# Layer one's tables: when the lists are loaded and made, and how the Q and P products are laid out

## The chip, the cores and the metric

The kernel runs on one core of a Trainium2 chip. The metric is the device time of one execution, in microseconds. The core has five engines that run their own instruction streams beside each other: TensorE (PE, matmuls and transposes into the eight PSUM banks), VectorE (DVE), ScalarE (ACT), GpSimd (POOL) and SyncE (SP, which here only issues DMAs). ACT and POOL issue DMAs as well. Streams meet only at semaphores.

## The reference

Two graph layers on 6250 nodes with 128 features and 206,250 edges sorted by destination. What matters here is layer one:

```python
h = x @ W1 + b1                                   # per node
e = concat([h[dst], h[src] - h[dst]])             # per edge
m = relu(e @ W2 + b2)
m = relu(m @ W3 + b3)
out = relu(segment_max(m, dst))
x = layernorm(x + out)
# layer two: per edge logit from dst and src, softmax over the edges of a node,
# weighted sum of projected rows, an MLP, a norm over the nodes, then
x = layernorm(x + layer_two(x, src, dst))
```

`e @ W2` splits into a part that depends on the destination alone and a part that depends on the source alone. So the kernel makes two tables of one row per node, P (for destinations, bias included) and Q (for sources), and an edge needs relu(P[dst] + Q[src]).

## The kernel before

**Tables (the first 80 us).** x is loaded in 13 steps of 512 rows (`load_x`, L280) by SP and ACT. For each step PE transposes four 128x128 blocks (`tr_x`, L763), ACT copies the result out of PSUM into one of two buffers `xTs` (L531), and PE multiplies it by a folded 128x256 weight `Wf`, whose left half gives P and right half Q (`mm_pq`, L772). DVE adds the bias on the way out of PSUM, four instructions of 128x256 for each step: Q goes to one of four buffers `qs`, P to its place in the large tile `accT` (`ev_pq`, L1064). SP stores Q step by step (L336), then P (L340). `accT` is later the accumulator of the layer, and is cleared at L1099.

**Lists.** The edges are cut into 1612 tiles of 128. `src` is loaded into S0 and `dst` into D, both with 124 partitions and 13 columns of 128 numbers (L458 to L460, L478 to L482, issued by POOL). DVE makes from D: `rel` (the place in the tile's window of 128 nodes), flags where a node starts and ends, `relend`, and five lists of bf16 numbers `metaS[0..4]` (L1074 to L1090). The lists go to DRAM (`lists_out`, L294: five stores, each 124 x 13 runs of 256 bytes; k = 0, 1 by SP, 2, 3, 4 by ACT). PE also turns three lists (`tr_list`, L782) and ACT keeps them in `srcT`, `relT`, `endT` (L537). `srcT` holds the indices of POOL's gathers.

**The edge loop.** 403 groups of four tiles. POOL gathers the Q rows of a tile (L489), SP loads the window of P for a tile (`windows`, L362) and, at two places of every 13 groups, spreads lists 0 and 1 over 128 partitions (`spread`, L368). PE adds both in PSUM (L806, L807), ACT applies relu, PE multiplies by W3 (L814), DVE runs a segmented maximum (L1110), PE picks the ends (L822, L831) and DVE adds into `accT` (L1128). SP enters the loop only after `meta_out` has reached 80 (all five lists stored), both tables are stored and all transposes of lists are done. Group k of POOL may run at most 13 groups ahead of PE.

Each engine's order is written by hand: `in_turn` runs stages step by step. In the first phase the order on DVE is: all 13 steps of `ev_pq` (with one cast of src behind step 2), then all the work on D, then the clearing of `accT`.

## Time and profile before

| what | value |
|---|---|
| median of 3 runs | 5077.51 us (5074.24 to 5079.42) |
| span of the profiled execution | 5109.1 us |
| busy: PE, POOL, DVE, ACT | 3054.7, 3094.9, 2392.0, 1577.1 us |
| first matmul of the edge loop | 125.46 us after the span's start |

The profiled execution is the only one that has a trace; the span from its first to its last instruction is 31.6 us longer than the median of the runs, so profiling adds some 0.6%. Times below are counted from the span's start. A row of the timeline gives start, duration, engine, line and operation, tiles, shape and count; the square brackets say how long the engine stood idle before and what ended that. A row whose engine ends in q (SPq, ACTq) is the engine's sequencer issuing a DMA: while it lasts nothing else of that engine's stream goes on. A DMA's landing is a separate time.

### The profile page before, as it was taken

How to read it: one execution, taken by the hardware profiler on the slowest of the kernel's cores; microseconds unless marked ns; L12 is line 12 of the kernel's file. 1: busy time of each engine (PE TensorE's matmuls, PEld its weight loads, DVE VectorE, ACT ScalarE, POOL GpSimd, SP SyncE). 2: the span in 40 equal slices, each digit the busy share in tenths (PEclk: the TensorE clock that was granted, in tenths of full speed). 3: DMA queues.
4: the chain of work that ended last, by engine and by line, in shares of the span. 5: the costliest groups of instructions: out<-in, count | busy, mean ns of one | idle time of the engine just before them, and what ended most of it. 6: DMA issues, size and time to landing. Idle time of an engine off the chain costs nothing.

```text
span 5109.1 us, 59978 instructions
## 1 busy us (share of the span) xinstructions
PE 3054.7 (60%) x16577; PEld 2440.6 (48%) x16577; DVE 2392.0 (47%) x7924; ACT 1577.1 (31%) x2413; POOL 3094.9 (61%) x3251
## 2 busy tenths in 40 slices
PE   3687777877777777777843444434444444444456
PEld 2566565666566665666612433333333333333343
DVE  3355444544544454444613444434444444444456
ACT  1344434444344444444522212212122221212214
POOL 4666666666666666666255666666666666666630
PEclk7888888888888898888865556666655555656567
DMA  6444444444444444444222222222222222222221
GB/s 154 133 138 134 130 128 140 134 127 133 138 129 124 146 132 125 141 129 131 81 77 58 68 74 69 75 68 68 75 67 75 68 68 74 68 71 72 68 67 53
DMA packets 407860, 512.07 MB, mean 100 GB/s; under 512 B 102789, under 2 KB 323495, under 8 KB 407527
## 3 DMA queue, kind: packets, MB, share of 16 engines
q1 hardware_dynamic: 292374, 288.47, 17.5%
q0 software_dynamic: 104832, 216.49, 17.1%
q10 hardware_dynamic: 10322, 3.28, 0.4%
q8 instruction: 135, 2.21, 0.2%
q14 instruction: 197, 1.61, 0.1%
HBM read 492.20 MB, written 15.68 MB: 99 GB/s over the span
## 4 chain that ended last, share of the span: by engine, by line
another core or an unknown queue 33%; PE 26%; issue 21%; ACT 10%; DVE 9%; DVEq 1%; DMA 1%; ACTq 1%; SPq 0%
PE bank L814 6%; PE bank L807 6%; PE bank L831 5%; DVE Z L1285 3%; PE bank L806 3%; PE bank L822 3%; ACT Z L639 2%; ACT Z L575 1%; PE bank L928 1%; ACT Z L570 1%; DVE Z L1274 1%; ACT Z L646 1%; DVE accT L1128 1%; ACT Z L582 1%
## 5 line engine op out<-in xcount | busy, mean ns | idle before, releaser
L489 POOL DMA_INDIRECT G<-q_tab,srcT x1612 | 1535.2, 952 | 892.1 <-issue 413.9
L489 POOL DMA_INDIRECT G<-x_tab,srcT x832 | 793.2, 953 | 478.1 <-issue 232.9
L1128 DVE TENSOR_TENSOR accT<-accT,bank 128x128 f32 x1612 | 454.5, 282 | 1166.6 <-remote 922.0
L489 POOL DMA_INDIRECT X<-x_tab,srcT x780 | 744.7, 955 | 380.3 <-issue 221.8
L807 PE MATMUL bank<-Z 128*128 128x128 f32 x3224 | 682.4, 308 | 103.0 <-issue 100.9
L928 PE MATMUL bank<-Z,G 128*128 128x128 f32 x1664 | 380.1, 396 | 554.4 <-DVE Z L1285 238.4
L928 PE MATMUL bank<-Z,X 128*128 128x128 f32 x1560 | 370.1, 406 | 523.1 <-DVE Z L1274 181.3
L1285 DVE SCALAR_TENSOR_TENSOR Z<-Z,evr,bank 128x128 f32 x1612 | 551.2, 342 | 195.4 <-issue 138.3
L807 PEld LDWEIGHTS bank<-Z 128*128 128x128 f32 x3224 | 576.9, 221 | 128.1 <-issue 127.8
L831 PE MATMUL bank<-Z 128*128 128x128 f32 x3224 | 520.9, 295 | 174.2 <-issue 168.4
L814 PE MATMUL bank<-Z,W3s 128*128 128x512 f32 x806 | 522.6, 736 | 156.1 <-issue 135.0
L928 PEld LDWEIGHTS bank<-Z,G 128*128 128x128 f32 x1664 | 323.0, 287 | 601.0 <-issue 411.2
L1274 DVE TENSOR_SCALAR Z<-iota,relT,evr 128x128 f32<-128x128 f32 x1612 | 563.6, 362 | 90.8 <-ACT evr L669 52.3
L806 PE MATMUL bank<-ident,G 128*128 128x128 f32 x1612 | 489.3, 304 | 165.3 <-issue 139.7
L928 PEld LDWEIGHTS bank<-Z,X 128*128 128x128 f32 x1560 | 314.1, 296 | 566.4 <-issue 317.7
L831 PEld LDWEIGHTS bank<-Z 128*128 128x128 f32 x3224 | 456.7, 209 | 189.0 <-issue 184.6
L1110 DVE TENSOR_TENSOR_SCAN Z<-Z,bank 128x512 f32<-128x512 bf16 x403 | 513.3, 1274 | 71.2 <-PE bank L814 66.7
L582 ACT ACTIVATE Z<-bank 128x512 f32<-128x512 f32 x403 | 239.6, 594 | 915.5 <-remote 651.9
L1116 DVE TENSOR_SCALAR Z<-iota,endT 128x128 f32<-128x128 f32 x1612 | 438.1, 296 | 0.0
L589 ACT COPY Z<-bank 128x512 f32<-128x512 f32 x403 | 234.5, 582 | 486.4 <-remote 298.2
L822 PEld LDWEIGHTS bank<-ident,Z 128*128 128x128 f32 x1612 | 237.0, 161 | 275.8 <-issue 274.6
L806 PEld LDWEIGHTS bank<-ident,G 128*128 128x128 f32 x1612 | 257.5, 160 | 209.6 <-issue 209.0
(198 smaller groups left out, 2982.5 us busy)
## 6 DMA issues: line engine op xcount, KB each, us to landing
Z<-p_tab SPq DMA_DIRECT2D x1612, 64.0 KB
Z<-meta SPq DMA_DIRECT2D x62, 896.0 KB
Z<-meta SPq DMA_DIRECT2D x61, 832.0 KB
Z<-meta SPq DMA_DIRECT2D x62, 768.0 KB
G<-q_tab,srcT POOLq DMA_INDIRECT x1612
G<-x_tab,srcT POOLq DMA_INDIRECT x832
X<-x_tab,srcT POOLq DMA_INDIRECT x780
x_tab<-X SPq DMA_DIRECT2D x13, 264.0 KB, 2.0
```

The costliest lines, as they stand in the source:

```text
L489: return pool.indirect_dma_start(to, None, of, bass.IndirectOffsetOnAxis(ap=srcT[:, t:t + 1], axis=0))
L806: nc.tensor.matmul(o, G[:, g * GT + j, 0:F], ident[:, :], start=True, stop=False, is_transpose=True)
L807: last = nc.tensor.matmul(o, Pwin[:, g * GT + j, :], OH[k % 3][:, j * 128:(j + 1) * 128], start=False, stop=True)
L814: nc.tensor.matmul(bank[2 + k % 2][:, :], W3s[:, :], M1[k % 3], start=True, stop=True).then_inc(v_mm, 1)
L822: last = nc.tensor.transpose(bank[4 + k % 2][:, j * 128:(j + 1) * 128], S[k % 3][:, j * 128:(j + 1) * 128], ident[:, :])
L831: last = nc.tensor.matmul(bank[6 + k % 2][:, j * 128:(j + 1) * 128], STs[k % 3][:, j * 128:(j + 1) * 128], EOH[k % 3][:, j, :], start=True ...
L928: last = nc.tensor.matmul(sum_bank(n)[:, j * 128:(j + 1) * 128], ring(t)[:, 1:F + 1], EW[n % (AHEAD + 1)][:, j, :], start=True, stop=True)
L1110: v.tensor_tensor_scan(out=S[k % 3], data0=bc[:, 1, g * CH:(g + 1) * CH], data1=bank[2 + k % 2][:, :], initial=NEG if k == 0 else S[(k - 1 ...
L1116: made = v.tensor_scalar(EOH[k % 3][:, j, :], iota_w, endT[:, k * GT + j:k * GT + j + 1], None, ALU.is_equal)
L1128: v.tensor_tensor(win, win, bank[6 + k % 2][:, j * 128:(j + 1) * 128], ALU.add).then_inc(acc_ok, 1)
L1274: made = v.tensor_scalar(EW[n % (AHEAD + 1)][:, j, :], iota_w, relT[:, t:t + 1], evr[:, q % 2, 0, at:at + 1], ALU.is_equal, ALU.mult)
L1285: v.scalar_tensor_tensor(out=win, in0=win, scalar=evr[:, q % 2, 1, w:w + 1], in1=sum_bank(n)[:, j * 128:(j + 1) * 128], op0=ALU.mult, op1= ...
```

## The change

- POOL no longer loads src at the start. It makes its constants first, then waits for x steps 0 to 6 and 8 (SP's) and 3 and 5 (ACT's), then loads src, then dst, then the 15 small weights that ACT loaded before.
- ACT copies every turned step of x into `accT` and keeps it there (`xt_of`); `xTs` is gone.
- PE makes 13 Q products (the right half of `Wf`) behind the transposes, then 13 P products (the left half) from the kept x. Four PSUM banks hold one product each.
- DVE takes each product out in one instruction of 128x512 into one of the four buffers `qs`; P uses the same buffers. SP stores all 26 in order.
- The work on D and S0 is cut into six pieces, each put behind one of the 26 steps of `ev_pq`. One tile `edge` holds the flags of starts and ends; ACT makes lists 0, 1, 2 and 4 from DVE's results, and subtracts 1 from `relend` when it keeps `endT`.
- ACT alone stores the five lists, in the order 0, 1, 2, 3, 4, between its other work.
- SP loads the `base` numbers before the stores of tables. It waits for the P stores one by one in the first 13 groups of windows, not for all ahead of the loop.

```diff
-            in_turn(STEPS, [(0, store_q)])
             with nc.allow_non_contiguous_dma(reason="one number for each tile"):
                 sp.dma_start(base[:, 0:TILES - 1], ...)
-            in_turn(STEPS, [(0, store_p)])
-            sp.wait_ge(prep, 6)
-            lists_out(sp, (0, 1))
+            def store(i):
+                tab, h = (q_tab, p_tab)[i // STEPS], i % STEPS
+                sp.wait_ge(pq_ev, i + 1)
+                sp.dma_start(tab[h * CH:(h + 1) * CH, :].rearrange("(p b) f -> p b f", b=SB), qs[i % 4]).then_inc(pq_out[i % 4], 16)
+
+            in_turn(2 * STEPS, [(0, store)])
             sp.wait_ge(meta_out, 80)
             sp.wait_ge(base_in, 32)
-            sp.wait_ge(p_out, 16 * STEPS)
 ...
             def windows(k, g):
+                if k < STEPS:
+                    sp.wait_ge(pq_out[(STEPS + k) % 4], (STEPS + k) // 4 * 16 + 16)
 ...
-            x_ready(pool, X_SP[-2])
-            x_ready(pool, X_ACT[-1])
+            pool.wait_ge(pads, 4)
+            x_ready(pool, X_SP[4])
+            x_ready(pool, X_ACT[1])
+            pool.dma_start(S0[0:ROWS, 0:COLS - 1, :], src[0:end].rearrange("(c p e) -> p c e", p=ROWS, e=T)).then_inc(src_in, 16)
 ...
+            pool.dma_start(W3s[:, :], W3[:, :]).then_inc(weights_in, 16)
 ...
                 act.wait_ge(xt_tr, h + 1)
-                after(act, pq_mm, h - 1)
-                nc.scalar.copy(xTs[h % 2], bank[h % 2][:, :]).then_inc(xt_cp, 1)
+                nc.scalar.copy(xt_of(h), bank[h % 2][:, :]).then_inc(xt_cp, 1)
 ...
+            act.wait_ge(prep, 2)
+            nc.scalar.copy(metaS[R, 0], rel[R]).then_inc(meta_ok, 1)
+            act.wait_ge(prep, 3)
+            nc.scalar.mul(metaS[R, 1], edge[R, :, 0:T], NEG).then_inc(meta_ok, 1)
+            act.wait_ge(meta_ok, 2)
+            lists_out(act, (0, 1))
+            nc.scalar.mul(metaS[R, 2], edge[R, :, 1:T + 1], NEG).then_inc(meta_ok, 1)
+            keep_list(1, lambda c, o: nc.scalar.copy(relT[:, c], o))
+            act.wait_ge(meta_ok, 3)
+            act.wait_ge(prep, 5)
+            lists_out(act, (2, 3))
             act.wait_ge(prep, 6)
-            lists_out(act, (2, 3))
-            act.wait_ge(prep, 7)
+            nc.scalar.copy(metaS[R, 4], S0[R]).then_inc(meta_ok, 1)
+            act.wait_ge(meta_ok, 4)
             lists_out(act, (4,))
+            keep_list(2, lambda c, o: nc.scalar.activation(endT[:, c], o, ACT.Identity, bias=minus))
 ...
-            in_turn(STEPS, [(0, tr_x), (1, mm_pqs)])
-            tr_list(rel, 1, 2)
-            tr_list(relend, 2, 5)
+            in_turn(STEPS, [(0, tr_x), (1, products)])
+            for i in range(STEPS, 2 * STEPS):
+                product(i)
+                if i == STEPS + 4:
+                    tr_list(rel, 1, 2)
+            tr_list(relend, 2, 4)
 ...
+            between = {6: numbers, 9: places_in_windows, 11: new_nodes, STEPS + 2: ends_of_nodes, STEPS + 5: other_nodes, STEPS + 8: places_in_blocks}
+
+            def ev_pq(i):
+                dve.wait_ge(pq_mm, i + 1)
+                after(dve, pq_out[i % 4], i // 4 * 16)
+                o = (128, 0)[i // STEPS]
+                v.tensor_tensor(qs[i % 4], blocks(bank[2 + i % 4][:, :]), bias[:, o:o + 128].unsqueeze(1).broadcast_to([128, SB, 128]), ALU.add).then_inc(pq_ev, 1)
+                if i in between:
+                    between[i]()
```

The new functions: `numbers` waits for src and casts it; `places_in_windows` waits for dst and makes `rel`; `new_nodes` makes `edge`; `ends_of_nodes` makes `relend`; `other_nodes` makes list 3 and `contS`; `places_in_blocks` masks dst for list 4. `product(i)` waits until product i - 4 has been taken out. `keep_list(n, keep)` is the old one with the instruction passed in; list 0 is now kept behind step 9 of x and not step 7.

How the instructions move on DVE, from the first product to the end of the work on the lists. Before, the last steps and what follows them (`Z<-bank` is an eviction to a Q buffer, `accT<-bank` one of P, `Z<-Z` the work on D and S0):

```order
L1064 TENSOR_TENSOR Z<-bank,brow 128x256 [waits q_out0,pq_mm]
L1064 TENSOR_TENSOR Z<-bank,brow 128x256
L1064 TENSOR_TENSOR accT<-bank,brow 128x256 x2
L1074 TENSOR_TENSOR Z<-Z 124x1664 [waits dst_in]
L1075 TENSOR_TENSOR Z<-Z 124x1664
L1077 CAST Z<-Z 124x1664 [waits prep,turns_dve]
L1078 TENSOR_SCALAR Z<-Z 124x1664
L1079 TENSOR_SCALAR Z<-Z 124x1664
L1081 TENSOR_SCALAR contS<-Z 124x13 [waits turns_dve]
```

Now, from step 6 to step 12 of the Q products:

```order
L1103 TENSOR_TENSOR Z<-bank,brow 128x512 [waits pq_out2,pq_mm]
L1075 CAST Z<-Z 124x1664 [waits src_in]
L1103 TENSOR_TENSOR Z<-bank,brow 128x512 [waits pq_out3,pq_mm]
L1103 TENSOR_TENSOR Z<-bank,brow 128x512 [waits pq_out0,pq_mm]
L1103 TENSOR_TENSOR Z<-bank,brow 128x512 [waits pq_out1,pq_mm]
L1079 TENSOR_TENSOR Z<-Z 124x1664 [waits dst_in]
L1103 TENSOR_TENSOR Z<-bank,brow 128x512 [waits pq_out2,pq_mm]
L1103 TENSOR_TENSOR Z<-bank,brow 128x512 [waits pq_out3,pq_mm]
L1082 TENSOR_TENSOR Z<-Z 124x1677
```

The work on dst stood behind all evictions, and now its first piece (L1079) stands ahead of the last three Q evictions and all those of P. The evictions are half as many and twice as wide.

On ACT, what stands between the last copy of x and the edge loop. Before:

```order
L531 COPY Z<-bank 128x512 [waits pq_mm,xt_tr] x5
L545 DMA W3s<-in_L_gnn_W 128x128
L550 DMA wprojs<-in_L_gnn_w_proj 127x128
...
L537 COPY relT<-bank 128x496 [waits list_tr] x3
L537 COPY relT<-bank 128x124 [waits list_tr]
L537 COPY endT<-bank 128x496 [waits list_tr] x3
L537 COPY endT<-bank 128x124 [waits list_tr]
L294 DMA meta<-Z 124x13x128 [waits prep]
L294 DMA meta<-Z 124x13x128
L294 DMA meta<-Z 124x13x128 [waits prep]
```

Now:

```order
L540 COPY accT<-bank 128x512 [waits xt_tr] x3
L556 CAST Z<-Z 124x1664 [waits prep]
L558 ACTIVATE Z<-Z 124x1664 [waits prep]
L295 DMA meta<-Z 124x13x128 [waits meta_ok]
L295 DMA meta<-Z 124x13x128
L561 ACTIVATE Z<-Z 124x1664
L562 COPY relT<-bank 128x496 [waits list_tr] x3
L562 COPY relT<-bank 128x124 [waits list_tr]
L295 DMA meta<-Z 124x13x128 [waits prep,meta_ok]
L295 DMA meta<-Z 124x13x128
L567 CAST Z<-Z 124x1664 [waits prep]
L295 DMA meta<-Z 124x13x128 [waits meta_ok]
```

The 15 loads of weights have gone to POOL. All five stores of lists stand on ACT, and the copies of `relT` stand behind the first two of them.

On POOL, the loads of src stood at its start. Now, behind its constants:

```order
L470 MEMSET X 128x52x3
L474 DMA Z<-in_src 124x12x128 [waits x_in3,x_in4,pads]
L475 DMA Z<-in_src 123x128
L476 DMA Z<-in_src 1x14x3
L477 DMA Z<-in_dst 1x3x43
L478 DMA Z<-in_dst 123x130
L479 DMA Z<-in_dst 124x11x130
L480 DMA Z<-in_dst 123x130
L481 DMA Z<-in_dst 1x43
L482 DMA W3s<-in_L_gnn_W 128x128
```

src and dst are now neighbours in one queue, and the loads of weights follow them.

## Rows read from the trace of the kernel before

**Rows 1.** The page: its span, and the group of POOL's gathers in layer one.
```profile
span 5109.1 us, 59978 instructions
L489 POOL DMA_INDIRECT G<-q_tab,srcT x1612 | 1535.2, 952 | 892.1 <-issue 413.9
```
**Rows 2.** Busy us in a stretch: PE, PEld, DVE, ACT, POOL; PE's granted clock.
```profile
1000.00:2000.00 1000.00, 770.83 (x4369) 610.02 (x4368) 494.04 (x1512) 408.02 (x671) 636.34 (x672) 0.87 0.45 133
```
**Rows 3.** The chain that ended last, to 130 us: start, duration, what.
```profile
3.95 21.66 DMA X<-in_x
...
128.26 15.34 issue
```
**Rows 4.** Timeline: work on lists, their stores, SP's next DMAs, the first matmul.
```profile
57.65 1.88 DVE L1074 TENSOR_TENSOR Z<-Z 124x1664 f32<-124x1664 int32 x1
...
72.91 15.12 SPq L294 DMA_DIRECT2D meta<-Z  x2
73.03 25.19 ACTq L294 DMA_DIRECT2D meta<-Z  x2
...
110.66 0.82 SPq L368 DMA_DIRECT2D Z<-meta  x2
...
125.46 0.45 PE L806 MATMUL bank<-ident,G 128*128 128x128 f32 x1 [52.80 <-issue]
```
**Rows 5.** Busy us in two stretches; the last number is DMA in GB/s.
```profile
8.00:10.00 2.00, 0.09 (x1) 0.00 (x0) 0.00 (x0) 1.50 (x2) 0.88 (x8) 1.00 1.18 311
...
12.00:14.00 2.00, 2.00 (x10) 1.68 (x9) 0.75 (x2) 0.61 (x2) 0.00 (x0) 1.00 1.41 116
```
**Rows 6.** Timeline: POOL's loads of src and dst, and the cast of src.
```profile
2.19 2.81 POOL L458 DMA_DIRECT2D Z<-in_src  x1 [0.65 <-DVE brow L1047]
...
34.53 1.05 DVE L1068 CAST Z<-Z 124x1664 f32<-124x1664 int32 x1
34.73 3.10 POOL L480 DMA_DIRECT2D Z<-in_dst  x1
...
38.36 0.51 POOL L482 DMA_DIRECT2D Z<-in_dst  x1
```
**Rows 7.** DMAs to 125 us: target, queue, count, KB each, us to landing.
```profile
q_tab<-Z SPq DMA_DIRECT2D x13, 256.0 KB, 4.8
...
Z<-in_src POOLq DMA_DIRECT2D x1, 744.0 KB, 17.4
...
Z<-in_dst POOLq DMA_DIRECT2D x1, 692.7 KB, 9.7
...
Z<-in_dst POOLq DMA_DIRECT2D x1, 0.2 KB, 14.5
```
**Rows 8.** POOL's queue from 20 to 28, then 44 to 52 us: packets, MB.
```profile
q0 software_dynamic: 82, 0.33, 19.8%
...
q0 software_dynamic: 131, 0.47, 16.5%
```
**Rows 9.** ACT's, SP's queue from 101 to 104; ACT's from 104 to 107 us.
```profile
q10 hardware_dynamic: 399, 0.10, 14.9%
q1 hardware_dynamic: 316, 0.08, 11.8%
...
q10 hardware_dynamic: 710, 0.18, 26.6%
```
**Rows 10.** Timeline: two evictions by DVE, one copy by ACT, a slow gather.
```profile
39.69 0.76 DVE L1064 TENSOR_TENSOR Z<-bank,brow 128x256 f32<-128x256 f32 x2 [0.75 <-PE bank L772]
...
40.13 0.59 ACT L531 COPY Z<-bank 128x512 f32<-128x512 f32 x1 [1.58 <-PE bank L763]
...
67.64 2.03 POOL L489 DMA_INDIRECT G<-q_tab,srcT  x1 [0.31 <-issue]
```
**Rows 11.** SP's loads of P windows, 113.5 to 147, then 147 to 165 us.
```profile
L362 SPq DMA_DIRECT2D Z<-p_tab x10: 13/698/710, 113.6 to 146.7; - x10
...
L362 SPq DMA_DIRECT2D Z<-p_tab x20: 3/332/697, 146.7 to 164.8; - x20
```

More of the change, by code:

```diff
@@ L136, in build @@
         S0 = z([COLS, T], i32)
-        srcF, rel, relend, flag = z([COLS, T]), z([COLS, T]), z([COLS, T]), z([COLS, T])
+        srcF, rel, relend = z([COLS, T]), z([COLS, T]), z([COLS, T])
+        edge = z([COLS, T + 1])
         metaS = z([5, COLS, T], bf16)
-        xTs = [z([CH]) for _ in range(2)]
+        W1T, Wf = z([128]), z([256])
+        top[0] = ZW - 4 * CH
         qs = [z([SB, 128]) for _ in range(4)]
-        W1T, Wf = z([128]), z([256])
         top[0] = 0
@@ L764, in tr_x, with product @@
                 last.then_inc(xt_tr, 1)
-            def mm_pq(h):
-                if h == 0:
+            def product(i):
+                which, h = divmod(i, STEPS)
+                if i == 0:
                     pe.wait_ge(fold_ok, 3)
                 pe.wait_ge(xt_cp, h + 1)
-                after(pe, pq_ev, 4 * h - 4)
+                after(pe, pq_ev, i - 3)
                 for b in range(SB):
-                    last = nc.tensor.matmul(bank[2 + h % 2 * 2 + b // 2][:, b % 2 * 256:(b % 2 + 1) * 256], xTs[h % 2][:, b * 128:(b + 1) * 128],
-                                            Wf, start=True, stop=True)
+                    last = nc.tensor.matmul(bank[2 + i % 4][:, b * 128:(b + 1) * 128], xt_of(h)[:, b * 128:(b + 1) * 128],
+                                            Wf[:, (128, 0)[which]:(256, 128)[which]], start=True, stop=True)
                 last.then_inc(pq_mm, 1)
@@ L1070, in _ @@
-            in_turn(STEPS, [(0, ev_pq)])
-            here, before, next_ = D[R, :, 1:T + 1], D[R, :, 0:T], D[R, :, 2:T + 2]
-            dve.wait_ge(dst_in, 16 * 5)
-            v.tensor_tensor(rel[R], here, D[R, :, 1:2].broadcast_to([ROWS, COLS, T]), ALU.subtract).then_inc(prep, 1)
-            chain(v.tensor_tensor(flag[R], here, before, ALU.not_equal))
-            dve.wait_ge(prep, 2)
-            v.tensor_copy(metaS[R, 0], rel[R])
-            v.tensor_scalar(metaS[R, 3], rel[R], 0.0, NEG, ALU.not_equal, ALU.mult)
@@ new lines, in places_in_windows, with new_nodes, ends_of_nodes @@
+            def places_in_windows():
+                dve.wait_ge(dst_in, 16 * 5)
+                v.tensor_tensor(rel[R], here, D[R, :, 1:2].broadcast_to([ROWS, COLS, T]), ALU.subtract).then_inc(prep, 1)
+            def new_nodes():
+                v.tensor_tensor(edge[R], D[R, :, 1:T + 2], D[R, :, 0:T + 1], ALU.not_equal).then_inc(prep, 1)
+            def ends_of_nodes():
+                dve.wait_ge(prep, 3)
+                v.scalar_tensor_tensor(out=relend[R], in0=rel[R], scalar=1.0, in1=edge[R, :, 1:T + 1], op0=ALU.add, op1=ALU.mult).then_inc(prep, 1)
@@ new lines, in other_nodes, with places_in_blocks @@
+            def other_nodes():
+                v.tensor_scalar(metaS[R, 3], rel[R], 0.0, NEG, ALU.not_equal, ALU.mult)
+                chain(v.scalar_tensor_tensor(out=contS[R, :], in0=rel[R, :, T - 1:T].rearrange("p c e -> p (c e)"), scalar=0.0,
+                                             in1=edge[R, :, 0:1].rearrange("p c e -> p (c e)"), op0=ALU.not_equal, op1=ALU.add))
+                v.tensor_scalar(contS[R, :], contS[R, :], NEG, None, ALU.mult).then_inc(prep, 1)
+            def places_in_blocks():
+                v.tensor_scalar(S0[R], here, 127, None, ALU.bitwise_and).then_inc(prep, 1)
```

108 lines of the change are left out of this document (42 added, 66 removed).

## The prediction

> **What bounds the kernel now.** I read the page first, then the chain of waits of the first 130 us, then the timeline and the DMA queues of the stretches that the chain names. On the page the thing to see is that POOL's 1612 gathers of layer one take 952 ns each [rows 1]; with about 0.3 us between two of them, four take 5.0 us. The edge loop runs 403 groups, its PE is busy 771 of 1000 us at a granted clock of 0.87, and POOL only 636 [rows 2]: POOL follows PE, and is no bound. So an earlier start of the loop should move everything behind it by the same amount, and the change touches nothing behind that start. All of its worth is in when the first groups run.
>
> The chain shows what the start waits for. First x: 21.66 us up to 25.6 [rows 3]. The products follow, then DVE's work on dst begins at 57.65 only, behind all evictions [rows 4]. The five lists are ready together: their stores are issued from 72.7 and 72.9 on, two by SP and three by ACT, and ACT's sequencer is held up to 98.2 [rows 4]. SP goes on at 110.66, when the last list has landed, and the first matmul of the loop starts at 125.46, 14.8 us later [rows 4]. Then PE has a hole of 15.34 us [rows 3] until group 1: SP issues P windows slowly there, 10 in 33 us, against 20 in the 18 us behind [rows 11]. The change alters neither these 14.8 us nor that code, so I shift both unchanged.
>
> **Part one: src behind x.** With src under way the DMA rate was 116 GB/s; just before, 311 [rows 5]. x is 3.2 MB, of which some 1.3 MB are in by 10 us at these rates. POOL's gate wants eight of the thirteen steps, 2.1 MB, but both queues move alike, so it opens when most of x is in: 10 + (3.0 - 1.3) MB / 311 GB/s = 15.5, say 16 us. The 21.66 us of x leave the chain. What is late next is src, and then dst.
>
> POOL issues src at 16 in some 3.9 us (2.81 for the large piece [rows 6], 0.5 for each small one), and dst behind it in about 5 (3.10 for the large one [rows 6]). Their 744 + 62 + 693 + 62 KB = 1.6 MB [rows 7] stand one behind the other in POOL's queue. That queue moved 0.47 MB in 8 us beside Q stores, 59 GB/s, and 0.33 MB in 8 us beside x, 41 GB/s [rows 8]. Data flow from about 19: at 59 GB/s dst is complete at 19 + 27 = 46, at 41 GB/s at 58. Before, the last piece of dst was issued at 38.36 and needed 14.5 us [rows 6, 7]: complete at 52.9, harmless since DVE looked at it at 57.65. I take 47, near the rate beside Q stores, which is the traffic that remains; bounds 43 and 58.
>
> DVE's cast of src stands behind Q step 6 and waits for it until about 34 (half of the 1.6 MB), and `rel` behind step 9 waits until 47. Each wait holds the evictions behind it, but PE may be three products ahead, so all transposes and all copies by ACT get through. These waits cost nothing by themselves: the lists need dst anyway.
>
> **Part two: half products, wide evictions.** An eviction of 128x512 is not in the trace. Below it lies one of the two halves, 0.38 us, above it the pair, 0.76 [rows 10]; I take 0.7. PE does the same columns as before. Stores set the pace of P: four buffers at 4.8 us to landing [rows 7] make 1.2 us a table, 16 us for 13. P begins at about 54, halts at step 5 while PE waits for ACT's copies of `relT` (below), and ends near 80, landed by 85. That is ahead of the last list, so it costs nothing; should stores take 7 us each, it would end at 95 and be level with it.
>
> **Part three: lists between the steps.** From dst at 47: `rel` 1.88 [rows 4], two evictions 1.4, `edge` 1.9 (as L1074), ACT's list 1. A cast of 124x1664 on ACT is not in the trace; DVE's takes 1.05 [rows 6], and ACT's 128x512 copy scaled by columns would give 0.59 x 3.25 = 1.9 [rows 10]; I take 1.5. Sum: the first list can be issued at 53.7, against 72.7. That is 19.0 us.
>
> **Part four: all five lists on ACT's queue.** The question is whether one queue takes 5/3 as long. From 101 to 104 both queues together moved 399 + 316 = 715 packets; from 104 to 107 ACT's alone moved 710 [rows 9]. So the two shared one limit of 240 packets a us, and 5 x 1612 = 8060 packets take 33.8 us on one queue too. Before, 110.7 - 72.7 = 38.0 us went by: 4.2 more, because stores of P filled the DMA engines first. Now 14 tables (Q step 12 and all of P) are stored beside the lists; 256 KB at 311 GB/s are 0.84 us each, 11.8 in all if nothing overlaps, 0 if all does. I take 8, nearer the upper end since the 4.2 were paid in full. End of lists: 53.7 + 33.8 + 8.0 = 95.5, against 110.7: **15.2 us earlier**.
>
> The Trainium skill (DMA: Bandwidth & Descriptors, section on why a DMA increments its semaphore by 16) says that a DMA is spread over the largest number of engines up to 16 that divides the outermost sizes; for 124 rows that is 4. It would explain why a second queue adds nothing; by it the sum stands as it is, and P stores would take only their share of those four engines. No row here names engines.
>
> Will ACT leave gaps in its queue? Its second issue holds it for 12 us (25.19 for two [rows 4]), to about 66. Only then come list 2, the copies of `relT`, PE's remaining transposes, and product 18, behind which DVE makes list 3: ready at some 70. Lists 0 and 1 keep the queue busy to 53.7 + 8 + 13.5 = 75 or, without interference, 67. So a gap of 0 to 3 us; I take 0. List 4 is made at 77, its turn comes after 81.
>
> **Part five: POOL.** 15 weight loads of about 0.5 us go ahead of the gathers, to about 33. The gathers wait for the last Q store, 47 + 6 + 0.7 + 4.8 = 59, against 64.4 before. At the loop's start POOL is 10 groups ahead instead of 12; at 5.0 us a group against PE's 5.7 that never comes to bear. A gather beside DVE's work on SBUF took 2.03 us against the mean of 0.95 [rows 1, 10].
>
> The Trainium skill (SBUF — State Buffer, "SBUF: two separate sides") explains it: a fast-mode DVE instruction locks GpSimd out of the port through which it writes descriptors. It speaks against giving POOL 15 more loads. By it the loads of src and dst might be issued 1 to 2 us later, and the sum would be 13 to 14 us.
>
> **Sum.** 15.2 us. The profiled span, 5109.1 [rows 1], would become 5093.9. It stands 31.6 above the median of 5077.51; I carry the microseconds over, not the ratio: **5062 us**.
>
> **Rivals.**
> (A) *The load of dst eats the gain.* src and dst share the engines with the rest of x and the Q stores and run at 41 GB/s: dst at 58, first list at 64.7, end at 64.7 + 33.8 + 11.8 = 110.3. Time: 5077, no change. For it: 41 GB/s was measured [rows 8]. Against: x is nearly done by then.
> (B) *Slower: one queue for five lists.* If the rate of 710 was a momentary one and a queue alone gives what each gave beside the other (399 in 3 us, 133 a us), 8060 packets take 61 us: end at 54 + 61 = 115, 4 us late, and with (A)'s late dst at 126: 5081 to 5093, say 5086. It decides below 8060 / (110.7 - 53.7) = 141 packets a us. Rows 9 are against it.
> (C) *The slow windows of SP go too.* If SP is slow for another reason than its code, such as POOL's free run of gathers, groups 0 and 1 may follow sooner; the hole of 15.34 us [rows 3] would shrink by up to 15: 5047.
> (D) *The shift is not kept*: something in the loop (SP's spreads, POOL) absorbs it, 5077. Rows 2 speak against it.
>
> **Chances.** Forecast 0.50, A 0.22, B 0.08, C 0.12, D 0.08. 0.2% (10 us) is about what a measurement of this kernel tells from no change. Own range of the forecast: 5054 to 5070; a quarter of it lies within 10 us of before. Faster: 0.375 + 0.12 + 0.035 of A and D = 0.53. Slower 0.10, same 0.37. The 8-in-10 range must take in A and most of C: 5048 to 5081.
>
> **What the changed profile would show.** x complete by 16 to 20; DVE idle ahead of the cast of src and of `rel`; the first store of a list at about 54 on ACT, the last landing near 95; SP's first spread then, the first matmul at 110, the next group some 18 later; POOL's gathers from 59. I am wrong if dst lands after 52, if ACT's queue moves under 200 packets a us without P stores beside it, or if the distance from last list to first matmul is not about 15.

## The result, and the profile after

Changed kernel: 5086.6 us median of 20 runs (5081.1 to 5101.3); before, beside it: 5077.6 (5072.0 to 5087.5, 20 runs). Ratio 1.0018, 95% interval 1.0012 to 1.0024: slower by 9 us, where 5062 was predicted. The time lies above the predicted range (5048 to 5081).

The page of after, the line that answers to [rows 1], and the window that answers to [rows 2]:

```profile
span 5085.5 us, 60170 instructions
L499 POOL DMA_INDIRECT G<-q_tab,srcT x1612 | 1531.9, 950 | 885.9 <-issue 423.3
```
```profile
1000.00:2000.00 1000.00, 776.12 (x4395) 610.27 (x4394) 496.49 (x1525) 411.85 (x677) 642.01 (x677) 0.87 0.44 134
```

Inside the loop nothing has changed. The chain of waits of after, its start (answers to [rows 3]):

```profile
6.89 9.21 DMA X<-in_x
...
20.27 22.59 DMA Z<-in_src
42.89 1.04 DVE Z L1075
...
58.43 12.07 issue
...
77.37 6.62 another core or an unknown queue
84.04 12.56 another core or an unknown queue
96.67 21.63 another core or an unknown queue
...
120.81 10.80 another core or an unknown queue
...
134.61 0.36 SPq L366
...
143.88 0.45 PE bank L819
```

x lets POOL go on at 16.1, as forecast. Then three things stand there that the prediction did not have: 22.6 us for src, 12.07 us in which PE waits, and 52 us in four pieces with no known releaser. The timeline of DVE in after shows what stands in the last four (L1103 is an eviction):

```profile
75.58 0.69 DVE L1103 TENSOR_TENSOR Z<-bank,brow 128x512 f32<-128x512 f32 x1 [14.71 <-PE bank L783]
...
84.01 0.69 DVE L1103 TENSOR_TENSOR Z<-bank,brow 128x512 f32<-128x512 f32 x1 [6.50 <-remote]
96.63 0.69 DVE L1103 TENSOR_TENSOR Z<-bank,brow 128x512 f32<-128x512 f32 x1 [11.93 <-remote]
118.32 0.69 DVE L1103 TENSOR_TENSOR Z<-bank,brow 128x512 f32<-128x512 f32 x1 [21.00 <-remote]
118.93 1.88 DVE L1095 TENSOR_SCALAR Z<-Z 124x1664 int32<-124x1664 int32 x1
131.63 2.49 DVE L1103 TENSOR_TENSOR Z<-bank,brow 128x512 f32<-128x512 f32 x4 [10.82 <-remote]
```

Five products of P (numbers 18 to 22 of the 26, counted from 0) reach DVE 8.4, 12.6, 21.7 and 13.3 us apart, and 7.3 us after POOL's first 52 gathers have ended (58.3 to 124.3) the rest come at once. These gaps are 12, 18, 31 and 19 times 0.70 us. PE itself was not late. Its timeline in after has the same five products in one row (each of their 20 multiplications shows as two), ended at 78.4:

```profile
71.59 6.79 PE L783 MATMUL bank<-Z,accT 128*128 128x128 f32 x40
```

The trace's semaphore updates say what was late. The last matmuls of products 19 to 22 were issued at 74.8, 76.3, 77.2 and 78.1, and the counter of finished products rose for them at 84.0, 96.6, 118.3 and 131.6. Up to product 17 it rose 0.3 us after each such issue. DVE's other wait, the one for a free buffer, was met at once each time (at 77.35, 84.02, 96.64 and 118.34). So neither PE's work nor a store held these evictions, but the signal of finished work. L1095, on which list 4 hangs, stands behind the product of 118.32; so list 4 is issued at 122.4 and SP enters the loop at 134.6.

The trace that stands ahead of the prediction comes from an execution 22 us longer than the longest of 20 timed runs. Profiling does not explain that: the profiled executions of the later kernels lie among their timed runs (after: 5087.2 beside a median of 5086.6). A later trace of the kernel before (before_third, below) has a span of 5071.5 us; so after is compared with that one:

| us from the start | before | after | in place (below) |
|---|---|---|---|
| first gather | 60.5 | 58.3 | 56.6 |
| last P product reaches DVE | 55 | 132 | 78 |
| SP enters the loop | 106.8 | 134.6 | 114.0 |
| first loop matmul | 122.1 | 143.9 | 127.0 |
| group 1 | 140.0 | 146.5 | 133.7 |
| group 10 | 189.0 | 198.8 | 182.7 |
| group 200 | 1313.9 | 1320.6 | 1306.8 |
| span | 5071.5 | 5085.5 | 5065.0 |

(One execution of a kernel differs from the next by more than the last rows can tell: the 20 runs of after span 20 us.) The start is 21.8 us late, but at group 1 only 6.5 are left. Before has a hole there, which after has not. SP's stretches of P windows in the timelines, first before (before_third), then after (start, duration, count at the end):

```profile
110.18 39.18 SPq L362 DMA_DIRECT2D Z<-p_tab  x18
```
```profile
136.46 13.96 SPq L360 DMA_DIRECT2D Z<-p_tab  x22
```

The chain of before_third shows how SP spent them until 143.1: one instruction each 0.70 us, whatever it was.

```profile
111.58 0.70 SPq L362
112.28 0.71 SPq L362
112.99 0.69 issue
```

POOL has a *free run* in both kernels: its first 13 groups, 52 gathers, wait for nobody. In before SP's slow windows lie beside this run (60.5 to 130.8, and four more gathers to 135.8) and the 7.3 us behind its last gather. In after SP comes to its windows when the run is over. So a first reading: *on this chip, whatever depends on PE's signals or on SP's instructions crawls while POOL gathers without pause.* Before had DVE's list work and the list stores there, which hardly need either; after has 8 P products and their stores there.

### The profile page after: what moved, and what is told of

It is laid out like the page before. It is cut to its first block, busy times and chain, and to the rows that moved or that the text cites. A ratio compares the mean times of both kernels' runs of the same rounds, so it can differ in the third digit from the quotient of the medians.

```text
span 5085.5 us, 60170 instructions
## 1 busy us (share of the span) xinstructions
PE 3040.6 (60%) x16681; PEld 2430.5 (48%) x16681; DVE 2386.0 (47%) x7892; ACT 1585.2 (31%) x2417; POOL 3096.1 (61%) x3267
## 3 DMA queue, kind: packets, MB, share of 16 engines
q1 hardware_dynamic: 289142, 287.65, 17.5%
## 4 chain that ended last, share of the span: by engine, by line
another core or an unknown queue 37%; PE 27%; issue 16%; ACT 12%; DVE 7%; DMA 1%; DVEq 1%; SPq 0%; POOL 0%; ACTq 0%; POOLq 0%
PE bank L827 6%; PE bank L820 6%; PE bank L844 5%; PE bank L835 3%; PE bank L819 3%; DVE Z L1304 3%; ACT Z L649 2%; ACT Z L585 2%; ACT Z L580 2%; ACT Z L656 1%; ACT Z L592 1%; ACT Z L599 1%; DVE Z L1293 1%; PE bank L941 1%
## 5 line engine op out<-in xcount | busy, mean ns | idle before, releaser
L819 PE MATMUL bank<-ident,G 128*128 128x128 f32 x1612 | 485.5, 301 | 112.6 <-issue 80.0
```

The source lines that it names most:

```text
L819: nc.tensor.matmul(o, G[:, g * GT + j, 0:F], ident[:, :], start=True, stop=False, is_transpose=True)
```

## The experiments

The runs fell on two kinds of chip: on some the kernel before takes 4304 us ("quick"), on others 5074 to 5131 ("slow"). The 20 runs of the result fell on a slow one. The mean granted clock (0.73 slow, 0.76 quick) differs by 4%, the time by 18%; the waits tell more. Whether it is the chip or a condition of it can't be told from here: the chip with number 4 in the record was quick in one batch (after_again) and slow in another 54 minutes later (src_first), if the number stands for the same chip both times. POOL's waits in 300 to 2000 us, in after on the slow chip, then in the same kernel on a quick one (us in total, times, longest):

```profile
POOL G L499 <- issue: 300.9, 980, 0.6
POOL G L499 <- remote: 266.7, 138, 2.2
POOL G L499 <- PE bank L820: 41.1, 32, 2.0
```
```profile
POOL G L499 <- issue: 410.3, 1346, 0.3
POOL G L499 <- PE bank L820: 4.6, 15, 0.3
```

On the slow chip POOL waits for PE; on the quick one it hardly does (4.6 us in 1700), and its own 4 x 1.25 us are the length of a group. Every time is told with its kind.

**Gathers held back (quick).** Theory one is the first reading. Theory two: the stores of lists and P, through the ring of four buffers, hold the products. Gathers behind all 26 table stores:

```diff
-                pool.wait_ge(pq_out[p], 16 * len(range(p, STEPS, 4)))
+                pool.wait_ge(pq_out[p], 16 * len(range(p, 2 * STEPS, 4)))
```


> The changed kernel, but POOL starts its gathers only when all 26 table stores have landed. Theory 1 (POOL's run of 52 gathers without a pause holds back PE's completions: the semaphore of the P products came 8.4, 12.6, 21.7 and 13.3 us apart between 75.6 and 131.6 us, and all those left at once after POOL had stopped at 124.3): the P products finish about 1 us apart, the last list lands near 95 instead of 131, the first matmul of the loop near 112 instead of 144; the time falls by 10 to 30 us against the changed kernel (5057 to 5077), unless the same run of gathers, now at 85 to 150, holds back the first groups of the loop instead. Theory 2 (list stores on ACT's queue or the ring of four buffers hold P back): the semaphore of the P products still comes 8 us and more apart, and the time stays within 5 us of 5086.

Measured 4332.7 (4331.8 to 4333.6), ratio 1.0064 (1.0048 to 1.0081). The same with `pool.wait_ge(meta_out, 80)` added:

> The changed kernel, but POOL starts its gathers only when all five lists have landed. Theory 1: nothing holds back the products; last list near 95, SP's spreads at 96, first matmul near 112; POOL is then only a few groups ahead, and has no run of 52 gathers without PE at work: 5050 to 5070. If POOL's lead of 12 groups is what the loop lives on, the first 50 groups run at POOL's 5.0 us and lose nothing, since PE takes 5.7. Theory 2: products still late, time near 5086 or above, since the gathers start later.

4341.3, ratio 1.0083 (1.0066 to 1.0100). In two parts (12 gathers, then `if k == 3: pool.wait_ge(meta_out, 80)`):

> The changed kernel, but POOL pauses after its first 12 gathers until all five lists have landed. Theory 1: the first 12 gathers take 15 us, from 58 to 73; in the trace of the changed kernel the completions were on time until 75.6, so nothing is held back: as with the gathers behind the lists, 5050 to 5070, with up to 3 us less since group 0 is there already. Theory 2: as the changed kernel, near 5086.

4327.4, ratio 1.0048 (1.0032 to 1.0065). And the kernel before with the wait for `meta_out` ahead of its gathers:

> The kernel before, but POOL starts its gathers only when all five lists have landed (110.7 us instead of 64.4). Theory 1: SP's slow issue of P windows (0.7 us an instruction from 112 to 146 us) and the hole of 15 us ahead of group 1 are also the gathers' doing, and shrink; the time falls by 5 to 20 us: 5058 to 5072. Theory 2, where the slow issue is SP's own code: the hole stays, and with no lead of POOL the time is the same or up to 10 us longer.

4342.6, ratio 1.0087 (1.0070 to 1.0104). All four landed on a quick chip, where their expectations (made for a slow one) could not be put to the test, and they say nothing of the slow one. On the quick one nearly each us that the gathers are held is lost. Then both kernels as they are, quick:

> The changed kernel once more, in company. The four kernels before this one ran on a chip where the kernel before takes 4304 us instead of 5077; there layer one goes at the pace of POOL's gathers (4.97 us a group in the traces; the times of the three kernels with held gathers and of the kernel before with held gathers are the start of the first gather plus 4238 to 4241). Theory 1 (two kinds of chip): on such a chip the changed kernel starts its gathers at 58.3 instead of 64.4 and is 4 to 8 us faster than before (ratio 0.998 to 0.999), and the semaphore of the P products comes 1 us apart; on a chip of the slow kind (near 5077) it is 5 to 13 us slower, and the P products' semaphore comes in steps of many us. Theory 2 (list stores or ring of buffers hold P back): the P products finish late on either kind, the time is longer than before on both.

4299.2 against 4304.7, ratio 0.9988 (0.9978 to 0.9998). The change *gains* 5 us there.

> The kernel before with a profile of its own on the same chip. On a chip of the quick kind: gathers from 64 us, first matmul of the loop near 117, no instruction of SP at 0.7 us, POOL never waiting for PE. On the slow kind: SP's spells at 0.7 us an instruction as in the trace at hand, and the first groups between 105 and 145 us.

4304.1, the first matmul of the loop at 122.2 and not near 117. DVE in after_again, the same products as above:

```profile
75.93 0.69 DVE L1103 TENSOR_TENSOR Z<-bank,brow 128x512 f32<-128x512 f32 x1
77.02 0.69 DVE L1103 TENSOR_TENSOR Z<-bank,brow 128x512 f32<-128x512 f32 x1 [0.40 <-PE bank L783]
77.91 0.69 DVE L1103 TENSOR_TENSOR Z<-bank,brow 128x512 f32<-128x512 f32 x1 [0.20 <-PE bank L783]
```

They come 0.9 us apart with the same stores and the same gathers beside them, so the stores alone do not hold them. But SP goes on at 107.7, not at the forecast 95.5: that part of the miss has nothing to do with the chip.

**What sets the time on a quick chip.** Three edits of when gathers can start, and after a third time.

```diff
+            sp.dma_start(S0[0:ROWS, 0:COLS - 1, :], src[0:end]...)   # behind load_x(sp, X_SP), POOL's loads of src gone
```


> SP loads src behind its part of x; POOL no longer loads it, all else as in the changed kernel. There the cast of src held DVE, and with it the Q evictions from step 7 on, from 25 to 43 us, because src came through POOL's queue. Theory (the time is the start of POOL's first gather plus a constant, 4298 - 58.5 = 4240 us on a chip of 4304, and 4.97 us a group behind it): src lands at about 27, the Q evictions go on from there, dst lands 5 to 10 us earlier, the first gather starts at 43 to 48 instead of 58.5, and the time falls by 10 to 15 us, to 4284 to 4289 (before: 4304). Rival (the end of the lists and the P stores sets the time): these end some 10 us earlier too, but the time then follows them and not the gathers, so gathers and time would move by different amounts. Rival (shift is absorbed behind the start of the loop): 4297 to 4300. On a slow chip (5077 before) the P products come to lie ahead of more of the gathers; there 5065 to 5075.

4307.0, ratio 1.0006 (0.9997 to 1.0016): a miss with its sign wrong. The timeline of src_by_sp says why:

```profile
11.49 0.42 SPq L339 DMA_DIRECT2D Z<-in_src  x1
11.96 20.78 SPq L340 DMA_DIRECT2D Z<-in_src  x1
...
45.08 14.18 SPq L350 DMA_DIRECT2D q_tab<-Z  x12
48.24 2.00 DVE L1104 TENSOR_TENSOR Z<-bank,brow 128x512 f32<-128x512 f32 x3 [28.07 <-DMA q_tab<-Z]
```

The large piece of src (744 KB, L339) was issued in 0.42 us, but the issue behind it, of the piece of 62 KB (L340), held SP's sequencer for 20.78 us. The stores of Q stand behind both and begin at 45.1, and DVE waits 28 us for a free buffer. First gather at 64.2, 6 later than in after, and the time is 6.6 longer.

```diff
-            between = {6: numbers, 9: places_in_windows, 11: new_nodes,
+            between = {6: numbers, STEPS - 1: places_in_windows, STEPS: new_nodes,
```


> The changed kernel with DVE's work on rel and edge behind the last Q eviction (steps 12 and 13) and not behind steps 9 and 11. The Q evictions no longer wait for dst nor for 1.9 + 1.9 us of DVE. Theory that gathers set the time on a chip of 4304: the first gather starts about 4 us earlier (54.5 instead of 58.5), the first list is issued 1 to 2 us later; time 4294 to 4296 against 4299. Rival (the lists set it): 0 to 2 us slower than the changed kernel, 4299 to 4301. On a slow chip: 5080 to 5088, no difference that can be told from the changed kernel.

4300.8, ratio 0.9990 (0.9980 to 1.0000): the first gather moves from 58.0 to 56.2, but the 52nd ends at 125.8 (125.3 in after_third, which ran beside it), since gathers now lie beside `rel` and `edge`; no gain, where 3 to 5 us were expected.

> The changed kernel again beside these. On a chip of 4304 us: 4299, ratio 0.9988, first gather at 58.5. On a slow chip (5077): 5087, ratio 1.0018, with the P products spread to 131 us.

4300.4, ratio 0.9989 (0.9979 to 0.9999). The gathers behind P a second time:

> The changed kernel, but POOL's first gather waits for all 26 table stores and not for the 13 of Q, so the P products run without gathers beside them. On a chip of 4304 us: 4333 again. On a slow chip, theory one (PE's completions lag while POOL gathers without pause, so that P products and lists end at 131 us): P products are through by 82, lists land by 108 and the loop starts at 120 instead of 144; the time is 5060 to 5087 there although the gathers start 30 us later. Theory two (the stores of lists hold the P products): P products still spread to 125 or more, and the time is 5087 or higher.

4331.2, ratio 1.0062 (1.0045 to 1.0079). All runs on quick chips, taken together:

| run | first gather | 52nd ends | first loop matmul | median | median less 52nd |
|---|---|---|---|---|---|
| before | 59.8 | 130.5 | 122.2 | 4304.1 | 4173.6 |
| after | 58.5 | 126.0 | 117.5 | 4299.2 | 4173.2 |
| after_third | 58.0 | 125.3 | 114.7 | 4300.4 | 4175.1 |
| rel_behind_q | 56.2 | 125.8 | 116.7 | 4300.8 | 4175.0 |
| src_by_sp | 64.2 | 131.6 | 120.9 | 4307.0 | 4175.4 |
| g_in_two | 57.6 | 151.3 | 111.1 | 4327.4 | 4176.1 |
| g_behind_p | 91.5 | 158.1 | 111.3 | 4332.7 | 4174.6 |
| g_behind_p_again | 88.7 | 155.0 | 109.7 | 4331.2 | 4176.2 |
| g_behind_lists | 103.5 | 168.3 | 112.5 | 4341.3 | 4173.0 |
| before_g_behind_lists | 105.1 | 169.9 | 114.4 | 4342.6 | 4172.7 |

The last column holds within 3.5 us while the median moves by 43; the first matmul of the loop goes its own way (111.1 with 4327.4, 122.2 with 4304.1). There the end of the 52nd gather sets the time. The change gains 1.3 us on the first gather and 3.2 on the run of 52.

**Part one undone (slow).** POOL loads src at its start; then also `rel` behind Q.

> Part one undone for src alone: POOL loads src at its start, as before the change; dst, weights, lists and products stay as in the changed kernel. Theory (time = end of the 52nd gather + 4175 us on a chip of 4304; that end follows the first gather): src is in by 20, x by 26 instead of 17.7, so the cast of src holds nothing. The evictions then wait for dst behind step 9; dst is half of what POOL's queue has behind the gate, in by 36 to 42. First gather at 46 to 52 instead of 58, time 4288 to 4294 (changed kernel 4300, before 4305). Rival (the wait for x in the chain, the 8 us that the change took out of it, is what sets the time): 8 us later than the changed kernel, 4308.

5141.2 against 5118.9, ratio 1.0046 (1.0029 to 1.0063).

> As src_first, and DVE's work on rel and edge stands behind the last Q eviction, so the Q evictions wait neither for src nor for dst. Theory: Q is stored by about 36 to 42 and the first gather starts there; 52 gathers end at about 106 to 112, and since the lists still land near 100 to 107 and PE starts 10 us later, the loop's start takes over as the bound: the 52nd gather no longer sets the time by itself. 4284 to 4292. Rival (the lists' end sets the time from the start, gathers only go along): no faster than src_first.

5140.7, ratio 1.0039 (1.0024 to 1.0053). Both miss: first gathers at 63.6 and 62.2, not at 46 to 52 and 36 to 42. With src ahead of it x opens POOL's gate at 34 to 35 and not at 16, and the stores of Q hold the evictions in the place of src (src_first_rel):

```profile
34.97 0.51 POOL L478 DMA_DIRECT2D Z<-in_dst  x1 [25.99 <-DMA X<-in_x]
...
39.00 2.13 DVE L1104 TENSOR_TENSOR Z<-bank,brow 128x512 f32<-128x512 f32 x3 [6.60 <-DMA q_tab<-Z]
```

In both the P products are spread again (12.7, 22.4 and 17.5 us apart in src_first), to 137, list 4 is issued at 139, and the first loop matmul comes at 158 and 159. The late gate speaks for part one, but that the changed kernel is slower still without it is not shown: it did not run beside these two, and its ratio on another slow chip (1.0028, 1.0018 to 1.0038, below) overlaps with theirs.

**Gathers held back (slow).** The test that tells the two theories apart, with the changed kernel beside it.

> The changed kernel with POOL's first gather behind all 26 table stores. In the traces of chips near 5080 to 5120 us, PE's signals to DVE for P products 19 to 22 came 12 to 22 us apart while POOL gathered without pause; at 4300 us they came 0.9 us apart. Theory one (on a slow chip PE's and SP's instructions crawl while POOL gathers without pause, and the change has moved the P products under that): here P products 19 to 26 come about 1 us apart and end by 85, list 4 is issued by 92 instead of 122 to 139, lists have landed by 108, the first loop matmul comes at 118 to 125 instead of 144 to 159; the time on a slow chip is 10 to 20 us under the changed kernel's unless the first groups then wait for gathers (they start 30 us later, which costs up to 25 us): 5070 to 5100 where the changed kernel has 5087 and before 5077. Theory two (stores of lists and of P hold the products): no difference in the products. On a quick chip: 4332 again.

> The changed kernel beside it. On a slow chip, ratio to before 1.002, first gather at 58, P products 19 to 22 spread over 40 us or more, first loop matmul at 144 to 159. On a quick chip 4300, ratio 0.999.

After: 5132.1 against 5117.3, ratio 1.0028 (1.0018 to 1.0038), P products 15.5, 22.4 and 15.4 us apart, first loop matmul at 153.2. With the gathers held: 5144.6, ratio 1.0059 (1.0042 to 1.0075). DVE in g_behind_p_third, the products that were spread, now three in 1.88 us:

```profile
72.95 0.69 DVE L1103 TENSOR_TENSOR Z<-bank,brow 128x512 f32<-128x512 f32 x1 [12.28 <-PE bank L783]
...
74.79 1.88 DVE L1103 TENSOR_TENSOR Z<-bank,brow 128x512 f32<-128x512 f32 x3
```

Lists and stores are all there, only the gathers are gone: theory two has fallen. The counter of products follows each last matmul by 0.3 us again (73.8 and 74.1 for product 19). A mixture, in which gathers delay the stores and the ring then holds the products, is ruled out by DVE's buffer waits in after, which were met at once. SP enters the loop at 102.9, 41 us before the changed kernel beside it does, the first matmul starts at 112.5. But the kernel is slower, for the free run (92.3 to 158.6) now lies beside the first groups:

```profile
104.45 73.95 SPq L360 DMA_DIRECT2D Z<-p_tab  x28
...
150.93 0.60 ACT L592 ACTIVATE Z<-bank 128x512 f32<-128x512 f32 x1 [30.30 <-remote]
```

SP needs 73.95 us for 28 windows (0.70 us an instruction until 8 us after POOL's last gather of that run), ACT waits 30.30 for PE's signal, and group 10 starts at 218.0 against 205.7. The slowness moved with the gathers, from the products to the loop. That shows by removal, and by return elsewhere, that the gathers' free run is the cause. It does not show what in the chip passes it on. An effect of profiling it is not: the profiled executions lie beside the other runs of their kernels (5145.2 beside a median of 5144.6, 5133.1 beside 5132.1).

**P ahead of the gathers.** What follows: a free run belongs beside work that needs neither PE's signals nor SP. P products are taken out in place, so that none waits for the ring, and the list work goes behind them.

```diff
+                if i < STEPS:
+                    after(dve, pq_out[i % 4], i // 4 * 16)
-                v.tensor_tensor(qs[i % 4], blocks(bank[2 + i % 4][:, :]), ...
+                v.tensor_tensor(qs[i % 4] if i < STEPS else blocks(xt_of(i - STEPS)), blocks(bank[2 + i % 4][:, :]), ...
-            between = {6: numbers, 9: places_in_windows, 11: new_nodes, STEPS + 2: ...
+            between = {6: [numbers], STEPS + 8: [places_in_windows], STEPS + 10: [new_nodes],
+                       2 * STEPS - 1: [ends_of_nodes, other_nodes, places_in_blocks]}
```

SP stores P from `accT`, the transposes of `rel` come behind all products, `accT` is cleared after the stores of P, and SP waits for these before the loop.

> A version built from the two findings. P products are taken out into the place of their own turned x in accT (as before the change), so no P eviction waits for a store; rel and edge stand behind P steps 8 and 10, the rest of the list work and the transposes of rel behind all P products; accT is cleared after the P stores. PE is through with the P products 13 x 1.06 = 14 us after the last Q product, at about 66, when POOL's free run of 52 gathers (from 54 to 56) has just begun. Lists are issued from 68. On a quick chip (before 4304, changed 4300) the time goes by the end of the 52nd gather + 4175: 123 to 125 gives 4298 to 4300. On a slow chip (before 5117, changed 5132): if PE's signals lag from the first gather on, the last P products come 12 to 20 us apart and the loop starts after 140, 5125 to 5140; if the P products get through, the lists land by 108 to 112, the loop starts at 120 to 127, and the time is at or below before, 5105 to 5117.

On a slow chip 5067.3 (5062.6 to 5072.3) against 5075.8, ratio 0.9985 (0.9976 to 0.9995). DVE in p_in_place:

```profile
59.41 0.69 DVE L1101 TENSOR_TENSOR accT<-bank,brow 128x512 f32<-128x512 f32 x1 [0.27 <-PE bank L781]
...
63.73 0.69 DVE L1101 TENSOR_TENSOR accT<-bank,brow 128x512 f32<-128x512 f32 x1 [2.16 <-PE bank L781]
...
77.99 0.69 DVE L1101 TENSOR_TENSOR accT<-bank,brow 128x512 f32<-128x512 f32 x1 [2.88 <-remote]
```

0.9 us apart until the first gather (56.6), then up to 4.3, the last at 78 instead of the expected 66, but not at 132. Group 1 follows the first by 6.7 us (17.9 in before), and the 6 us at group 10 stay to the end (table above). Again, with a second trace of before:

> The version with P taken out in place again. On a slow chip (before 5076 to 5119): ratio 0.9985 again, first gather at 57, last P product at 78, loop from 127. On a quick chip (before 4304, changed 4300), where the time is the end of the 52nd gather + 4175: gathers from 56 or 57, the 52nd ends at 124 to 126, 4299 to 4301, ratio 0.999.

5067.8 against 5074.4, ratio 0.9985 (0.9974 to 0.9996).

> The kernel before beside it, for a second trace of it on the same chip. On a slow chip (the first trace of before was 22 to 31 us longer than the timed runs): span 5070 to 5120, first gather at 60 to 64, all products through before it, first loop matmul at 122 to 126, group 10 at 180 to 193. On a quick chip 4304.

5073.3, span 5071.5; the table above uses it. The version differs from after in several things at once (in place, list work later, transposes later, SP's wait for all P stores); which of them carries the gain was not taken apart. It was never run on a quick chip.

**The small pieces first (slow).** Of the 16.8 us that DVE waits for src, is 12 us the last piece of 0.2 KB?

```diff
-            pool.dma_start(S0[0:ROWS, 0:COLS - 1, :], ...            # 744 KB, then 62 KB, then 0.2 KB
+            pool.dma_start(S0[ROWS - 1:ROWS, COLS - 1, ...           # 0.2 KB, then 62 KB, then 744 KB
```

This stands on top of p_in_place, and the pieces of dst are turned round in the same way.

> p_in_place with POOL's loads of src and dst in another order: the small pieces (0.2, 62 KB) ahead of the large one of each. In the traces of the changed kernel and of p_in_place the large piece of src lands 11.9 us after its issue, at 28.8, but the piece of 0.2 KB that is issued third takes 22.6 us, to 42.9, behind the large piece of dst, and it alone ends the wait of 16.8 us for the cast. Theory: src is complete at 30 to 31, the cast runs there, the Q evictions go on 12 us earlier, the first gather starts at 45 to 50 (p_in_place: 56.6), the last P product is through by 60 to 66, the last list lands by 102 to 106 (114). Slow chip: loop from 114 to 118 (127), time 5056 to 5063 (before 5075, p_in_place 5067). Quick chip: end of the 52nd gather at 114 to 118 + 4175 = 4289 to 4293, if the loop's start (108 to 112) does not take over. Rival: POOL's queue moves no faster, and the small pieces only exchange the wait with the large one, which then lands at 42: no difference to p_in_place, ratio 0.9985 or 0.999.

5124.2 against 5130.6, ratio 0.9987 (0.9978 to 0.9997), as p_in_place: the rival was right. The issues of src to 60 us, in after, then in small_first (KB each, us to landing):

```profile
Z<-in_src POOLq DMA_DIRECT2D x1, 744.0 KB, 11.9
...
Z<-in_src POOLq DMA_DIRECT2D x1, 0.2 KB, 22.6
```
```profile
Z<-in_src POOLq DMA_DIRECT2D x1, 744.0 KB, 26.0
...
Z<-in_src POOLq DMA_DIRECT2D x1, 0.2 KB, 8.1
```

The wait only changed hands: all of src is there 26 to 27 us after POOL's first issue, whatever the order.

## Why the prediction was wrong, step by step

- **Part two, the step that failed.** "P ... ends near 80, landed by 85. That is ahead of the last list, so it costs nothing." The pace of P was worked out from stores and from PE's columns. What it lies beside was left out: POOL's free run, from 58.3. On the slow chip P reached DVE at 132 and SP could store the last at 134. On the quick chip, where no signal is late, the last eviction of P ended at 87 and no list waited for one (what the stores of P cost there is in part four). The rows for it stood in the trace of before: SP's 10 windows in 33 us [rows 11] and the hole of 15.34 us [rows 3], both beside the free run and the few us behind it. The prediction put them down to SP's code and carried them over unchanged; only rival C asked whether the gathers made them.
- **How much is whose.** SP was to go on at 95.5 and went on at 134.6. Of these 39.1 us 12.2 are there on the quick chip too, where SP goes on at 107.7 (3.0 from part three, 9.2 from part four, below); the other 26.9 came on the slow one alone and are put down to the late signals. So without them the 15 us would not have come either: on the quick chip SP enters the loop 4.9 us before the kernel before does (112.6).
- **Rival C came true and was not enough.** First matmul to group 1: 17.9 us before, 2.6 after, 15.3 less, as C had it ("by up to 15"). The main term went the other way: the loop starts 21.8 us later, not 15.2 earlier. 21.8 - 15.3 = 6.5 at group 1; 9.8 at group 10, 9.0 in the medians.
- **Rival B named the right number by chance.** It said 5086, and 5086.6 was measured. Its mechanism, a single queue at 133 packets a us that ends the lists at 115 to 126, is not what happened: in after ACT's queue moved the first four lists by 94, then had nothing to move until list 4 was issued at 122.4.
- **Part one.** x right (16.1). The gate and the issue of src right (16.9 to 20.8). src was complete at 42.9 instead of 34, because its last piece and dst share POOL's queue; dst at 46.0 (forecast 47). "These waits cost nothing by themselves" was wrong: 16.8 us of DVE's waiting put Q's end at 55 and all of P behind that, under the gathers.
- **Part three.** First list issued at 56.5, not 53.7. The eviction of 128x512 took 0.69 us (0.7 taken), ACT's cast 1.58 (1.5).
- **Part four, mis-sized on both chips.** 41.8 us from first issue to last landing were forecast: 33.8 for the packets and 8 for the stores of P beside them. Quick: 56.7 to 107.7, 51.0 us, so 17.2 in place of the 8. That ACT's queue would have no gap was right. ACT's second issue held its sequencer for 12 us, as forecast. List 3 came later than forecast (PE waits for ACT's copies of `relT`, the 12.07 us of the chain, so product 18 came at 74, and lists 2 and 3 were issued at 76, on the quick chip), but lists 0 and 1 kept the queue busy until then. What was wrong is the rate. ACT's queue in after_again from 60 to 68, 72 to 76, and 84 to 88 us (packets, MB, share of the engines):

```profile
q10 hardware_dynamic: 978, 0.25, 15.5%
...
q10 hardware_dynamic: 1000, 0.26, 28.4%
...
q10 hardware_dynamic: 370, 0.09, 10.9%
```

  These are 122, 250 and 92 a us. Stores of P are under way in the first and the third stretch, gathers in all three: so beside the stores of P the rate falls under half, and beside the gathers alone it does not. The mean is 8060 / 51.0 = 158 a us, not far above the 141 below which rival B was to decide. Slow: list 4 waits for the eviction of 118.32; lists end at 131, SP goes on at 134.6.
- **Part five.** First gather at 58.3 (59 forecast). The 15 loads of weights cost nothing: they ended at 33.9, and POOL then waited 24.4 us. "POOL follows PE, is no bound" is right on the slow chip and wrong on the quick one. A gather beside DVE's work on lists: first in before_again, then in after_again.

```profile
61.92 2.64 POOL L489 DMA_INDIRECT G<-q_tab,srcT  x1 [0.30 <-issue]
64.87 2.04 POOL L489 DMA_INDIRECT G<-q_tab,srcT  x1 [0.30 <-issue]
```
```profile
60.44 0.96 POOL L499 DMA_INDIRECT G<-q_tab,srcT  x1 [0.30 <-issue]
61.71 0.95 POOL L499 DMA_INDIRECT G<-q_tab,srcT  x1 [0.30 <-issue]
```

  This is the 3.2 us of the quick chip: the change takes DVE's work from beside the first gathers (what the 52 take beyond 0.95 us each is 5.8 us in before_again and 2.6 in after_again). The Trainium skill (SBUF — State Buffer, "SBUF: two separate sides") has a fast DVE instruction lock GpSimd out of their shared port. The trace agrees in that gathers take up to 2.64 us beside DVE's work on lists and 0.95 without it; whether that work ran in such a mode no trace shows. For POOL's loads, of which the prediction feared it, there was no test: src's large piece took 2.82 us against 2.81, but DVE only took products out of PSUM or stood idle meanwhile.
- **The sum.** It started from an execution that was 31.6 us above the median, and carried microseconds over. That did no harm to the difference, but its hole at group 1 and its 110.7 were taken as fixed (before_third has SP's entry at 106.8).

## What to carry to other kernels

When a step is moved, ask not only whether it is done in time, but what it will now lie beside: here 8 cheap products were moved under a 66-us run of gathers, and on the slow chip four of their signals came 8 to 22 us apart instead of 1. A stretch that is slow "for no reason" in the profile (a sequencer that takes the same 0.70 us for every instruction) is a cause to be found before the change, not a constant to be carried over. And a time is not one number for a program: what bounds it (on the quick chip the end of the 52nd gather, on the slow one not, since there POOL waits for PE) can change with the chip, and a change of 0.2% can be a gain on one and a loss on the other.

## What the runs showed of the hardware

- One program took 4304 us on some chips and 5074 to 5131 on others. In 1000 to 2000 us a group took 5.0 us on the quick ones and 5.9 on the slow, at a granted clock of 0.91 and 0.87. POOL was busy for 3.8 us of a group on both; what is added on the slow one is its wait for PE (267 us in 1700, 0.9 us a group). PE's busy time a group went from 3.9 to 4.6 us. What bounds the group there was not taken apart.
- On the slow ones, while POOL issued indirect gathers without a pause, SP took 0.70 us an instruction and PE's signals came at multiples of 0.70 us, with PE's work done up to 53 us before its signal (after, product 22). On quick ones no such stretch was seen. It began soon after the first gather (in p_in_place product 17's signal, 3 us into the run, was 2 us late; the gaps over the first 20 us were 1.5 to 4.3 us, later 8 to 22 in after), and it ended 7.3 us after the last gather of the run in after and in before_third, 8 us after it in after_fourth and g_behind_p_third. What is slow there was not found.
- Behind a DMA of 1488 runs of 512 bytes (744 KB), itself issued in 0.42 us, the next issue on SP's queue, of 62 KB, held the sequencer for 20.78 us (src_by_sp). ACT's second list store behind a first of 1612 runs of 256 bytes held it for 11.3 us in after. What stood behind on the same engine waited as well (the stores of Q, the copies of `relT`).
